# First batch of a two-layer attention kernel: parts and stacks sent ahead of a fill with zeros, by two queues, and constant products on TensorE whose result nobody reads

## The reference, cut to what matters

```python
x = x + attn(layernorm(x))     # layer A, 16 heads of 8 columns (values: 32)
x = x + ffn(layernorm(x))      # layer F, 8 heads of 64, 8 experts

def attn(x):                   # x is 8 x 512 x 128
    Q, K, V = heads(x), heads(x @ Wk + bk), heads(x @ Wv + bv)
    o = softmax(Q @ K^T + causal) @ V
    return x + gelu(o) @ Wf + bf

def ffn(x):
    q, k = x @ w_q, x @ w_k
    sel, gm = argmax, one-hot of sigmoid(x @ w_gate)     # one expert per token and head
    values = x @ value_experts[sel], times its gate
    out = causal softmax(q @ k^T / 8) @ values
    return sum over heads of output_experts[sel] of out
```

## Time and profile before

| | us |
|---|---|
| runs, median of 3 | 1242.96 (1241.27 to 1246.39) |
| the profiled execution | 1249.98 |
| its span, first to last instruction | 1248.2 |
| PE busy | 1125.7 (90%) |
| ACT busy | 945.1 (76%) |
| DVE busy | 864.1 (69%) |
| POOL busy | 363.9 (29%) |
| mean granted clock of TensorE | 0.957 |

### The profile page before, as it was taken

The page is one execution under the profiler, slowest core; times in us unless marked ns, Lnnn a source line. Parts: engine busy times, 40 slices in busy tenths (PEclk is TensorE's granted clock), DMA queues, the critical chain, the costliest instruction groups (busy, mean ns, idle before and its releaser), DMA issues.

```text
span 1248.2 us, 19900 instructions
## 1 busy us (share of the span) xinstructions
PE 1125.7 (90%) x5720; PEld 636.2 (51%) x5720; DVE 864.1 (69%) x2715; ACT 945.1 (76%) x2639; POOL 363.9 (29%) x460
## 2 busy tenths in 40 slices
PE   2697998999989999999989999899999999899998
PEld 1124754357543764347543575437643475435753
DVE  4732878658676687758786686767877597866844
ACT  3874788956989489867889669894898678896651
POOL 1012323242133322342232421343223332323210
PEclk8556999989999999999999999999999999999999
DMA  6201223002320222202230023202222032300220
GB/s 192 67 10 71 69 84 90 11 15 69 111 59 12 58 65 78 59 4 69 86 95 10 20 65 111 59 12 60 64 77 59 4 75 85 91 3 24 56 69 9
DMA packets 43646, 72.73 MB, mean 58 GB/s; under 512 B 9664, under 2 KB 25408, under 8 KB 43216
## 3 DMA queue, kind: packets, MB, share of 16 engines
q1 hardware_dynamic: 42256, 67.26, 20.1%
q10 hardware_dynamic: 1280, 4.20, 1.2%
HBM read 45.34 MB, written 8.80 MB: 43 GB/s over the span
## 4 chain that ended last, share of the span: by engine, by line
PE 42%; ACT 30%; DVE 14%; issue 8%; DMA 3%; SPq 2%; POOL 2%; ACTq 0%; DVEq 0%
ACT masked L899 14%; PE ps_m L679 10%; ACT pt L950 10%; PE ps_o L667 8%; DVE masked L1275 6%; PE ps_max L576 3%; PE ps_exp L576 3%; PE ps_max L788 2%; PE ps_exp L578 2%; PE ps_m L485 2%; ACT s2k L839 2%; DVE val L1468 2%; POOL pt L1142 2%; ACT s2q L839 1%; DVE pt L1449 1%
## 5 line engine op out<-in xcount | busy, mean ns | idle before, releaser
L899 ACT ACTIVATE masked<-masked,low 128x512 f32<-128x512 f32 (+3 forms) x768 | 422.8, 553 | 73.3 <-DVE low L1275 71.6
L1275 DVE CUSTOM_DVE_ANT_0 masked<-ps_max,mask 128x512 f32<-128x512 f32 (+3 forms) x768 | 350.1, 487 | 158.0 <-PE ps_max L576 90.7
L1142 POOL TENSOR_SCALAR_AFFINE_SELECT pt<-pt 128x512 f32<-128x512 f32 (+2 forms) x192 | 144.8, 754 | 560.9 <-ACT pt L950 560.9
L950 ACT ACTIVATE pt<-ps_exp 128x384 f32<-128x384 f32 (+1 forms) x480 | 238.3, 517 | 63.4 <-PE ps_exp L576 35.4
L667 PE MATMUL ps_o<-pt,val 128*32 128x128 f32 (+6 forms) x1536 | 188.0, 471 | 15.4 <-POOL pt L1142 15.4
L576 PE MATMUL ps_max<-s2k,s1q 72*128 72x512 bf16 (+3 forms) x512 | 129.7, 321 | 49.6 <-DVE low L1275 29.3
L679 PE MATMUL ps_m<-at,oe_sb 128*128 128x512 f32 x300 | 157.6, 612 | 1.9 <-DVE at L1326 1.9
L899 ACT ACTIVATION_READ_ACCUMULATOR masked<-masked,low 128x1 f32 x768 | 146.1, 190 | 0.0
L576 PEld LDWEIGHTS ps_max<-s2k,s1q 72*128 72x128 bf16 x512 | 47.0, 99 | 144.7 <-DVE low L1275 72.1
L1326 DVE TENSOR_TENSOR at<-osb,hots 128x512 f32<-128x512 f32 x150 | 104.3, 700 | 14.0 <-PE ps_m L679 14.0
L576 PE MATMUL ps_exp<-s1q,s2k 75*128 75x384 bf16 (+3 forms) x384 | 99.2, 323 | 11.4 <-ACT pt L950 8.6
(11 more groups left out here) (183 smaller groups left out, 1960.8 us busy)
## 6 DMA issues: line engine op xcount, KB each, us to landing
hots<-hot_d SPq DMA_DIRECT2D x48, 256.0 KB, 4.5
s1q<-parts_q SPq DMA_DIRECT2D x96, 96.0 KB
s2k<-parts_k SPq DMA_DIRECT2D x96, 96.0 KB
s1q<-pt SPq DMA_DIRECT2D x64, 128.0 KB, 2.3
s1k<-pt SPq DMA_DIRECT2D x64, 128.0 KB, 2.3
hots<-hot_d ACTq DMA_DIRECT2D x16, 256.0 KB, 4.5
parts_q<-pt SPq DMA_DIRECT2D x24, 128.0 KB, 2.3
parts_k<-pt SPq DMA_DIRECT2D x24, 128.0 KB, 3.8
```

What stands on the lines that cost most here:

```text
L899: last = nc.scalar.activation(e, e, ACT.Exp, bias=low[:, g % 2, c:c + 1], scale=-1.0, accum_out=den[:, g % 2, c:c + 1])
L950: nc.scalar.activation(pt[:, (n % 2) * 4 + j, 0:c1 - c0], score_bank(k, u)[:, c0:c1], ACT.Exp).then_inc(exp_done[k].sem, 1)
L1142: nc.gpsimd.affine_select(out=v, in_=v, compare_op=ALU.is_ge, fill=0.0, base=0, pattern=[[0, HG[k]], [0, m], [1, P]], channel_multiplier=- ...
L1275: last = v.tensor_tensor_reduce(out=masked[:, u % JUNK, c0:c0 + w], in0=src[:, c0:c0 + w], in1=mask[:, S - w:S], scale=-1.0, scalar=POS, o ...
```

## The change

Two things are done to batch 0, and nothing to the other batches.

First, the fill of `s2q` with zeros moves on SP from ahead of the parts to behind all stacks. The wait for the three small DRAM tables (`cst`) moves to the point where they are first read. The k stack of group 0 with its rows of ones is issued by ACT (`first_keys`), once it has made the high halves of the expert weights; SP issues the rest. TensorE no longer waits for the zeros; SP (ahead of `one_rows`) and ACT (ahead of `experts`) do, late in the batch.

Second, TensorE gets products of two constants, `wf_sb` and the identity, into bank 1 (`ps_m[1]`), which nobody reads. Six of 512 columns stand ahead of layer A, one of 256 columns behind each of the 36 units of the first stage, and one of 512 columns at each place where a later batch does a product of the batch before: 12 in the second stage, 9 in the turn. The wait for `w_in[1]` (the load of `wf_sb` among others) moves ahead of them.

```diff
-            sp.wait_ge(cst.sem, cst.count(0, 16 * 3))
-            sp.dma_start(s2q[0:64]...zeros_d[0].partition_broadcast(64)).then_inc(zero_rows.sem, 16)
...
             parts_to_dram(0, "q")
-            sp.wait_ge(zero_rows.sem, zero_rows.count(0, 16))
             parts_to_dram(0, "k")
+            sp.wait_ge(cst.sem, cst.count(0, 16 * 3))
...
             for g in range(GROUPS):
                 restack_q(g)
-                restack_k(g)
+                if g > 0:
+                    restack_k(g)
+            sp.dma_start(s2q[0:64]...zeros_d[0].partition_broadcast(64)).then_inc(zero_rows.sem, 16)
             for b in range(B):
                 layer_a(b)
+                if b == 0:
+                    sp.wait_ge(zero_rows.sem, zero_rows.count(0, 16))
                 one_rows(b)
...
+            def idle_product(columns):
+                mm(ps_m[BANK["F", "acc", 0]][:, 0:columns], ident_sb[:],
+                   wf_sb[:].rearrange("p g d -> p (g d)")[:, 0:columns], start=True, stop=True)
             def product(f, u):
+                if f < 0:
+                    idle_product(S)
+                    return
...
                         if a > 0:
                             outputs(a - 1, "pre", n)
+                        else:
+                            idle_product(IDLE)
...
-                            if a > 0 and OUTPUTS.get(("A", u)):
+                            if OUTPUTS.get(("A", u)):
                                 outputs(a - 1, "A", u)
-                            elif a > 0 and u == PRODUCT_AT:
+                            elif u == PRODUCT_AT:
                                 product(a - 1, T * E - TURN - 1)
...
-                if a > 0:
-                    product(a - 1, T * E - TURN)
+                product(a - 1, T * E - TURN)
...
-            pe.wait_ge(zero_rows.sem, zero_rows.count(0, 16))
             pe.wait_ge(set_v.sem, set_v.count(0, 3))
             pe.wait_ge(set_p.sem, set_p.count(0, 2))
+            pe.wait_ge(w_in[1].sem, w_in[1].count(0, 16 * 3))
+            for n in range(FIRST_IDLE):
+                idle_product(S)
...
+            def first_keys():                     # on ACT
+                act.wait_ge(cst.sem, ...); act.wait_ge(parts_out["k"].sem, ...)
+                three DMAs of ks, one of its rows of ones, on ACT's queue
...
             expert_weights_high()
+            first_keys()
```

More of the change, by code:

```diff
@@ L106 @@
 SCORES_AT = 10
+FIRST_IDLE, IDLE = 6, 256
 def pre_groups(a):
@@ L329, in _ @@
             sp.dma_start(wf_sb[:], wf.rearrange("p (g d) -> p g d", d=D)).then_inc(w_in[1].sem, 16)
-            sp.wait_ge(cst.sem, cst.count(0, 16 * 3))
-            sp.dma_start(s2q[0:64].bitcast(F32).rearrange("p h n -> p (h n)"), zeros_d[0].partition_broadcast(64)
-                         ).then_inc(zero_rows.sem, 16)
             def parts_to_dram(a, name):
@@ L466, in _ @@
                 restack_q(g)
-                restack_k(g)
+                if g > 0:
+                    restack_k(g)
+            sp.dma_start(s2q[0:64].bitcast(F32).rearrange("p h n -> p (h n)"), zeros_d[0].partition_broadcast(64)
+                         ).then_inc(zero_rows.sem, 16)
             for b in range(B):
                 layer_a(b)
+                if b == 0:
+                    sp.wait_ge(zero_rows.sem, zero_rows.count(0, 16))
                 one_rows(b)
@@ L795, in turn @@
                 f, first = a - 1, T * E - TURN
-                if f >= 0:
-                    product(f, first + 1)
+                product(f, first + 1)
                 project_back(a, (0, 1, 2))
-                if f >= 0:
-                    product(f, first + 2)
+                product(f, first + 2)
                 project_back(a, (3,))
-                if f >= 0:
-                    for u in range(first + 3, T * E - 2):
-                        product(f, u)
+                for u in range(first + 3, T * E - 2):
+                    product(f, u)
                 transposed("F", a)
-                if f >= 0:
-                    product(f, T * E - 2)
-                    product(f, T * E - 1)
+                product(f, T * E - 2)
+                product(f, T * E - 1)
             pe.wait_ge(w_in[0].sem, w_in[0].count(0, 16 * 4))
@@ L816, in _ @@
                 value_a(0, t)
-            pe.wait_ge(zero_rows.sem, zero_rows.count(0, 16))
             pe.wait_ge(set_v.sem, set_v.count(0, 3))
             pe.wait_ge(set_p.sem, set_p.count(0, 2))
+            pe.wait_ge(w_in[1].sem, w_in[1].count(0, 16 * 3))
+            for n in range(FIRST_IDLE):
+                idle_product(S)
             for b in range(B):
                 attention_a(b)
-                if b == 0:
-                    pe.wait_ge(w_in[1].sem, w_in[1].count(0, 16 * 3))
                 turn(b)
@@ L1089, in expert_weights_high @@
                 copy(ve_h[:], ve_raw).then_inc(split_hi.sem, 1)
+            def first_keys():
+                act.wait_ge(cst.sem, cst.count(0, 16 * 3))
+                act.wait_ge(parts_out["k"].sem, parts_out["k"].count(0, 16 * PARTS))
+                n_rows, h = PARTS * DH, slice(0, HG["A"])
+                for m in range(PARTS):
+                    nc.scalar.dma_start(ks[m * n_rows:(m + 1) * n_rows, h],
+                                        parts_d["k"].rearrange("m d h n -> (m d) h n")[:, h]
+                                        ).then_inc(restacked_a[0].sem, 16)
+                nc.scalar.dma_start(ks[STACK:STACK + PARTS, h], onesb_d.rearrange("p (h n) -> p h n", n=S)[:, h]
+                                    ).then_inc(restacked_a[0].sem, 16)
             nc.scalar.preload_act_table_set(EXP_LN)
@@ L1105, in _ @@
                 turn(b)
+                if b == 0:
+                    act.wait_ge(zero_rows.sem, zero_rows.count(0, 16))
                 experts(b)
```

## The result

| | before | after |
|---|---|---|
| median, us | 1243.82 (1241.27 to 1246.39, 4 runs) | 1228.82 (1227.51 to 1233.78, 4 runs) |
| ratio | | 0.9873, 95% interval 0.9841 to 0.9904 |
| profiled execution, us | 1249.98 | 1233.78 |
| its span | 1248.2 | 1232.1 |
| mean granted clock | 0.957 | 0.993 |

The change makes the kernel 15.0 us faster (12 to 20 by the interval); 19.2 were forecast, 1224 against a measured 1228.8, inside the range of 1216 to 1234. The forecast of where the time goes holds; three of its sizes do not.

The account below looks back on a forecast made before the run. In batch 0, ACT bounds the first stage and half-clocked PE the second. Terms -8.0 + 0.5 - 9.2 - 0.5 - 2.0 = -19.2 us give 1230.8 profiled, 1223.8 for the median, range 1216 to 1234.

Parts of the forecast that it names:

- Rival (a): Batch 0: the clock stays at half and the products are only extra work; +37 us, 1280 us; chance 0.05.
- Rival (b): Start of batch 0: stacks come only at 30 us, sharing engines with group 1's q stack; 3.3 less gained, 1227; chance 0.10.
- Rival (d): Second stage, batch 0: ACT's order holds it at 44 us; 2.7 gained there instead of 9.2, 1230; chance 0.06.
- Start: Start of batch 0: first unit at 26.7 us instead of 34.71; 8.0 us gained, bounds 4.7 and 9.7.
- near the unchanged chain less a bit: Start of batch 0: reason for taking 26.7 us, where the unchanged chain from k's parts to the first unit gives 27.4.
- that rule: Start of batch 0: a second queue saves issue time alone; start would be 27.4 us, the sum 0.7 us smaller.
- The zeros: Batch 0: sent behind group 3 around 32 us, landing some 7 us later, needed only behind the turn; free.
- Six products ahead: Before layer A, batch 0: two or three run at half clock, they end at 24 to 26 us, start not delayed.
- Rival (c): Batch 0: clock rises but falls again, in stretches or the pause before the stacks; 3 to 7 us less gained; chance 0.14.
- First stage: Layer A, batch 0: +0.5 us for a late rise or a product in a unit's way; bounds -1 and +4.
- Second stage: Layer A, batch 0: PE's list becomes batch 2's, 37.5 us instead of 46.65; 9.2 gained, bounds 5.9 and 11.6.
- Turn and front: Batch 0: turn gains 0.5 us (bounds -0.5 and 1), front of layer F 2.0 (bounds 0 and 2.5).

Follow-up runs that it names:

- The start alone: The changed kernel without any of its constant products, so TensorE's list is that of before; median 1234.12 us, ratio 0.9913 to before.
- the products alone: The constant products as in the changed kernel, but SP's and ACT's lists as before, zeros first; median 1238.34 us, ratio 0.9946 to before.
- one queue: The changed kernel with SP, not ACT, issuing group 0's k stack and rows of ones; median 1231.37 us, ratio 0.9892 to before.
- group 1 held: The changed kernel, but SP waits until group 0 has landed before issuing any stack of group 1; median 1231.57 us, ratio 0.9900 to before.
- the twelve: The changed kernel with twelve constant products ahead of layer A instead of six; median 1228.66 us, ratio 0.9871 to before.
- the second execution of before: The unchanged kernel profiled once more for a second look at its clock; 1242.34 us (one run), second stage 40.49 us.
- changed again: The changed kernel, nothing altered, run and profiled once more; median 1228.95 us, ratio 0.9876 to before.

## Why the prediction was right, and where its sizes were off

**What bounds batch 0** was read rightly: ACT the first stage, PE at half clock the second. The start alone and the products alone give 11.1 and 6.9 us, each clear of noise, so there are two gains. Their sum, 18.0, is 3 more than the 15.0 of both, within the intervals; that they add exactly is not shown. By L568 the two together give 19.2 against 16.7 to 18.0 measured from the first execution of before, and 9.8 against 12.0 to 13.3 from the second. Rival (a), the products as mere extra work, fell: with them the second stage has clock 1.00, without them it took 44.05 us at half clock for most of its length. Rival (b), the stacks at 30 us behind group 1, came true in kind only: they came at 27.63, and holding group 1 back brings 1.5 to 1.9 us, not 3.3. Rival (d), ACT's order holding the second stage at 44, fell: 37.38 us against 37.5 forecast.

**Start:** 8.0 us forecast, 7.1 measured (27.63; 27.27 in the second execution), 27.4 if nothing but the parts' departure counted. The parts were in DRAM at 18.87 against the 18.3 forecast, since those of k took 3.6 us to land and not 2.3. The term "near the unchanged chain less a bit" failed in the bit: I gave the second queue 0.7 us, and one queue is just as fast. That was not for lack of an early ACT: it sent k at 18.87, sooner than the 19.32 I gave it. The q stack of group 1 takes some of it back, as holding it showed; how much is open, for no run held group 1 with one queue. As DMA: Bandwidth & Descriptors of the Trainium skill ("Rules for kernel authors") has it, two queues share the engines and save only issue time. The traces agree: 27.11 us with one queue, 27.27 and 27.63 with two. Weighed in the prediction and priced at 27.4, that rule was the better guess.

**The zeros,** put at nothing and at 7 us to land, took 16 to 20 us in ten executions, and by the timing they held up the last of the rows of maxima. In the two executions of the changed kernel that left 0.9 us to spare and cost PE a wait of 0.3; with group 1 held back it cost a wait of 4.4.

**Six products ahead:** the forecast had the clock rise among them and no delay. It was up before them, at 16 us, and no delay came. What was missed is what came behind: with the six over at 22.2 and the stacks at 27.6, PE paused for 5.4 us and the clock fell. The forecast had them end at 24 to 26, counting products at half clock. Rival (c) named this pause, with 3 to 7 us; it costs 1 to 2, shown by the twelve, which remove it.

**First stage:** +0.5 forecast, +2.0 and +1.1 measured, within the bounds of -1 and +4. The products in the units' way cost nothing at full clock (27.21 us).

**Second stage:** -9.2 forecast, -9.3 measured between the two profiled executions. This is the term that was mis-sized for the median. The 46.65 us of the one execution before were a long case; another took 40.49, which makes the gain 3.1, and the start alone had 43.41. The sum by stages is 7.1 - 2.0 + 9.3 + 0.3 + 2.1 = 16.8 against the first execution and 8.9 - 1.1 + 3.1 + 0.3 + 2.1 = 13.3 between the two second ones; the medians differ by 15.0, between the two. The prediction had said that if timed runs already have some of the clock in batch 0 they gain up to 3.7 us less; it should have been in the forecast and not only in the range, for the profiled execution was 7 us above the median of the runs. Of the 5.0 us between the forecast of 1223.8 and the measured 1228.8, 0.9 is only that the median of before is 1243.82 in the measured set and not 1242.96.

**Turn and front:** -0.5 and -2.0 forecast, -0.3 and -2.1 measured.

**Behind L568** the instructions are the same. Single half-clock stretches turn up in other batches in most executions, in batch 1 before, in batches 2 and 4 after, but none in the second execution of before and none in the start alone. Whether the change has a part in them is not shown. They carry part of the spread: from L568 to the end it took 1113.5 and 1110.6 us in the two executions of before, 1114.0 and 1110.5 in those of the changed kernel, and 1107.0 with the start alone.

Still open is whether the 42 products of the first stage are worth anything; their own set of runs would have to tell 0 from 4 us.

## What to carry to other kernels

Where TensorE is full and its clock is still low, look at what kind of work fills it: a few dense products that nobody needs can pay for themselves. Here 12 of them, 10.4 us of TensorE, took the stage that TensorE bounds from 44.05 to 37.4 us; the 42 in and ahead of the stage before it are not shown to be worth anything. Before sizing such a gain, compare the profiled execution with the median of the runs: if it is slower, part of what it shows is a bad case, and the forecast should be cut by it. A transfer that is needed first should leave first, and a fill that is needed last can go behind it. But look at what small transfer is issued next: here 4 KB rows of maxima landed behind 1 MB of zeros, and holding back the next group to speed up the first only moved the wait to them.

## What the runs showed of the hardware that was not expected

- A nearly full TensorE stayed at half clock: 26.3 busy of 28 us, clock 0.50, with bf16 scores of 72 rows and 32-column products. With 12 f32 products of 128x512 on the whole array among the same work the granted clock was 1.00 over 37.4 us, in five executions. It is no guarantee: batch 1 of before has such products too, and fell to 0.52 for 7 us.
- The time at which the clock rises in such work varies from execution to execution, at 86 and at 104 us in two executions of the same kernel, and the second stage with it, 40.49 to 46.65 us. Over the timed runs of before, the fastest, 1237.59 us, had a mean clock of 0.972, and the slowest, 1250.80, one of 0.960; the highest clock, 0.973, belongs to a run of 1238.85 us and the lowest, 0.958, to one of 1247.35.
- With the same matmuls up to there, the clock first rose at 16.0 us in one execution of the changed kernel and at 17.5 in the other, by the spacing of its 512-column matmuls (0.43 us, then 0.23); in the two executions of before it rose at 17.4, and not yet at 17.5.
- A DMA on ACT's queue left at 18.87 us while the activation ahead of it in ACT's program ran from 16.69 to 20.30; in the second execution of the changed kernel the same, 18.66 within 16.50 to 20.10.
- A small transfer can land behind a large one issued long before it: the last `mt_a` DMA took 6.7 to 12.1 us where 1 MB of zeros stood ahead of it on the queue, and landed 0.4 to 0.6 us behind the zeros in three executions (changed, changed again, group 1 held), while the two DMAs ahead of it took 2.3 to 5.1 us. In the two executions of before and in the products alone, where the zeros go first, none took over 2.2.
- The stack of group 0 (588 KB in seven DMAs of rows of 1 KB) takes from its first issue to the last landing 8.7 us with two queues (18.87 to 27.6), 8.3 with one (18.85 to 27.1), and 7.3 when nothing follows it (18.4 to 25.7).
